# A hybrid of eight residual layers: the third normalization merged into linear attention, and the rings of PSUM tiles changed in two kinds of feed-forward

## Chip, cores, metric

The kernel runs on one core of one Trainium2 chip. The metric is the device time of one execution in microseconds (us), lower is better; a time given for the kernel is the median of several runs.

## The reference, cut to what matters

The input x has 8 sequences of 512 tokens with 128 channels. Eight residual layers follow, each on a layer normalization of x. The change touches the second, third, fourth, sixth and eighth:

```python
x = x + L0_attn_a(layernorm(x))          # state space scan
x = x + L0_ffn(layernorm(x))             # quantized feed-forward
x = x + L0_attn_b(layernorm(x))          # linear attention
x = x + L0_ffn(layernorm(x))
x = x + L1_attn_a(layernorm(x))          # forgetting attention
x = x + L1_ffn(layernorm(x))             # einsum with sign(weight)
x = x + L1_attn_b(layernorm(x))          # rotary attention
x = x + L1_ffn(layernorm(x))

# L0_ffn: every product of fp4_linear quantizes its input in blocks of 16
scale = max(abs(xb)) / 6; q = grid[searchsorted(mid, abs(xb / scale))] * sign * scale
h = silu(fp4_linear(x, w_gate)) * fp4_linear(x, w_up); y = fp4_linear(h, w_down)   # 128 -> 352 -> 128
# L0_attn_b: no softmax
att = (0.1 * x @ Wq) @ (0.1 * x @ Wk).T; att = att * causal - (1 - causal)
att = att / (sum(att) + 1e-5); y = att @ (x @ Wv) @ Wo + bo
```

## The kernel before

x lives in SBUF for the whole kernel as X, channels on the 128 partitions, [batch, token] along them. The program is a row of stages, one after the other. Each `Stage` opens its own SBUF and PSUM tiles and semaphores, and ends with clearing the semaphores and a barrier of all engines; inside it each engine runs its instructions in the order in which the code writes them, and waits on semaphores alone. No planner and no pool decides anything. All data here are 32-bit floats; such a matmul shows as two records on PE (TensorE). PSUM has eight banks of 512 floats a partition, and each stage divides them by hand.

`layernorm_stage`: `center(n)` is a matmul with I - 1/128 for batch n into a ring of six banks, `keep(n)` copies it to XN on VectorE (DVE), ScalarE (ACT) squares it; `variance(k)` brings four batches' means into one bank, 32 rows each; ScalarE's `root(k)` and VectorE's three-step `refine(k)` make `fine`, 1/sqrt; `widen(k)` spreads it to all channels with four matmuls of 32 rows, and VectorE's `scale(n)` multiplies XN by it.

`linear_attention_stage`: for each of the 8 batches PE computes `tokens_up`, `values`, four blocks of `scores`, `outputs` and `turn` (a transpose). ScalarE copies from PSUM, GpSimd (POOL) puts -1 where a token must not look, VectorE divides by the row sum and adds the residual. PE's order interleaves batch i's outputs with batch i+1's scores.

`ffn0_stages` works on tokens on the partitions. Its front normalizes and quantizes X: a pair of batches is 1024 floats a partition, so two banks. Three such places make the ring `cps`, two more banks are `qps`. `center(g)` is called for g = 0 to 3 (the statistics: `moments` on ScalarE, `block_maxima` on VectorE) and a second time for g = 4 to 7, since three places can't hold four pairs until their scales are known. Then each pair goes through `code_scaled`, `sizes` (ScalarE), `code_total`, `minus_code`, GpSimd's product (line 1018), `back` (transposes on PE) and `out` into XQ. The last call waits for a place:

```python
for g in range(BATCHES + RING):
    center(g)
center(BATCHES + RING)
back(0)
back(1)
```

The main loop then runs over 16 pairs of 128-token tiles: `gates`, `ups_of` on PE, `product`, `maxima`, `scales`, `scaled`, `total` on VectorE, sizes on ScalarE, two pairs of products on GpSimd (lines 1023, 1026), `turn` and `down` on PE, and a `residual` on VectorE in every other pair from the sixth on. gates, ups and transposes take the ring's PSUM again.

`norm_ffn1_stage` never stores the normalized x: `center(n)` into one of two banks, a square on ScalarE, `variance`, `root`, `refine`; meanwhile `signed(n)`, a matmul with the centered sign matrix `mix`, into the same two banks, `keep(n)` on ScalarE copies it, `widen(k)` spreads four batches' 1/sqrt over four banks, VectorE's `scale(n)` multiplies and GpSimd adds to X. In the last stage SP (the DMA queue) sends X out by twos.

## Time and profile before

| | us |
|---|---|
| median of 3 runs (2116.9 to 2118.9) | 2117.75 |
| the profiled execution's own time | 2115.72 |
| its span in the trace | 2113.9 |
| first quantized feed-forward, from its first matmul to the next stage's first | 381.1 to 509.4 |
| third normalization | 509.4 to 529.5 |
| linear attention | 529.5 to 594.3 |
| second quantized feed-forward | 594.3 to 721.1 |
| sign-mixed stages | 1708.7 to 1738.4 and 2082.6 to the end |

Times in the trace are us from the span's start. A stage starts where the one before has ended on all engines, so what a stage saves the kernel saves, and waits inside one stage do not reach into another.

### The profile page before, as it was taken

What the parts mean: (1) busy time and instruction counts of PE and PEld (TensorE: products, weight loads), DVE (VectorE), ACT (ScalarE), POOL (GpSimd) and SP (SyncE); (2) the same over time, 40 slices, a digit from 0 to 9 for tenths busy, and PEclk for the clock granted to TensorE, in tenths of its full rate; (3) what the DMA queues carried; (4) which work ended last, traced back from release to release, by engine and by line L of the source; (5) the groups of instructions that cost most, each with busy time, mean ns of one, the idle gap of its engine ahead of it and who ended that gap; (6) DMA issues with size and microseconds to landing.
All of it is one profiled execution on the core that took longest, in us unless ns stands there. A gap on an engine that the chain in (4) does not pass through costs nothing. (4 is left out here: it accounts for less than half of the span.)

```text
span 2113.9 us, 36196 instructions
## 1 busy us (share of the span) xinstructions
PE 1808.2 (86%) x11955; PEld 870.2 (41%) x11955; DVE 1683.8 (80%) x2282; ACT 1404.3 (66%) x2314; POOL 1042.6 (49%) x1138
## 2 busy tenths in 40 slices
PE   4558887687978769999999999999999867789996
PEld 2213332543764314555555555555554423222222
DVE  5979997796369669888888888888887637798884
ACT  2547775575357547777777777777776534789994
POOL 0067775174217435776666666776666521431112
PEclk9869999798999879999999999999999979999999
DMA  3000000000000021111121111112121100422211
GB/s 98 0 15 0 0 0 0 1 1 1 2 1 1 0 74 49 59 60 61 54 63 64 60 54 61 64 60 61 53 63 63 37 16 25 96 83 52 61 46 40
DMA packets 71437, 84.54 MB, mean 40 GB/s; under 512 B 20544, under 2 KB 44032, under 8 KB 71168
## 3 DMA queue, kind: packets, MB, share of 16 engines
q1 hardware_dynamic: 69536, 81.69, 12.8%
q8 instruction: 94, 1.54, 0.3%
q10 hardware_dynamic: 1728, 0.67, 0.1%
q14 instruction: 79, 0.65, 0.1%
HBM read 71.95 MB, written 9.57 MB: 39 GB/s over the span
## 5 line engine op out<-in xcount | busy, mean ns | idle before, releaser
L1806 DVE SCALAR_TENSOR_TENSOR fu_kv<-fu_ps_kv,fa_vec,fu_kv 128x511 f32<-128x511 f32 (+2 forms) x384 | 285.8, 746 | 55.7 <-ACT fu_kv L1678 50.7
L1889 POOL TENSOR_TENSOR fu_ds<-fu_p 128x768 f32<-128x768 f32 x64 | 115.8, 1809 | 191.6 <-PE fu_ps_ss L1577 191.4
L2244 ACT ACTIVATE rt_p<-rt_ps_s 128x1024 f32<-128x1024 f32 x192 | 185.6, 1029 | 25.1 <-PE rt_ps_s L2175 25.1
L1537 PE MATMUL fu_ps_s<-fu_qn,fu_kn 64*128 64x512 f32 (+3 forms) x1024 | 190.0, 468 | 2.2 <-DVE fu_sg L1767 1.4
L625 POOL TENSOR_TENSOR scan_hC<-scan_h,scan_c 128x1024 f32<-128x1024 f32 x64 | 150.9, 2358 | 71.7 <-DVE scan_h L601 71.7
L1678 ACT ACTIVATE fu_kv<-fu_ps_kv,fa_vec 128x512 f32<-128x512 f32 x128 | 88.3, 690 | 110.9 <-PE fu_ps_kv L1586 67.0
L1567 PE MATMUL fu_ps_n<-fu_p,fu_vt 128*64 128x512 f32 (+3 forms) x1024 | 151.9, 439 | 0.0
L524 PE MATMUL scan_ps_y<-scan_hC,w_ident 128*128 128x512 f32 x256 | 125.8, 614 | 26.3 <-POOL scan_hC L625 14.8
L601 DVE TENSOR_TENSOR_SCAN scan_h<-scan_dA,scan_ps_b 128x1024 f32<-128x1024 f32 x64 | 146.4, 2287 | 2.2
L2140 POOL TENSOR_SCALAR rt_d<-rt_d 128x1024 f32<-128x1024 f32 x32 | 35.0, 1094 | 184.0 <-DVE rt_d L2265 178.3
L1905 POOL TENSOR_TENSOR fu_kn<-fu_ks,fu_rb 128x512 f32<-128x512 f32 x64 | 81.6, 1275 | 71.0 <-DMA fu_rb<-rms_rows 70.7
L1682 ACT ACTIVATE fu_ps_kv<-fu_kv 128x512 f32<-128x512 f32 x128 | 77.0, 602 | 55.8 <-DVE fu_kv L1806 55.6
L1537 PEld LDWEIGHTS fu_ps_s<-fu_qn,fu_kn 64*128 64x128 f32 x1024 | 82.9, 185 | 74.6 <-issue 55.7
L571 ACT ACTIVATE scan_c<-scan_ps_c 128x1024 f32<-128x1024 f32 x64 | 65.6, 1024 | 67.4 <-PE scan_ps_c L545 49.1
L2189 PE MATMUL rt_ps_o<-rt_p,rt_va 128*32 128x512 f32 x768 | 103.3, 610 | 7.0 <-ACT rt_p L2244 5.6
L567 ACT ACTIVATE scan_dA<-ssm_delta,w_decay 128x511 f32 (+1 forms) x128 | 85.1, 716 | 13.2 <-DVE scan_dA L587 13.0
L2175 PE MATMUL rt_ps_s<-ra_stackq,ra_stackk 48*128 48x512 bf16 x512 | 84.5, 391 | 6.3 <-PEq L75 5.7
L1567 PEld LDWEIGHTS fu_ps_n<-fu_p,fu_vt 128*64 128x64 f32 x1024 | 63.4, 136 | 63.4 <-issue 60.2
L1909 POOL TENSOR_TENSOR fu_num<-fu_num,fu_sg 128x512 f32<-128x512 f32 x64 | 82.6, 1291 | 9.9 <-DVE fu_sg L1767 9.8
L1893 POOL TENSOR_TENSOR fu_ds<-fu_ds,fu_p 128x512 f32<-128x512 f32 x64 | 82.3, 1285 | 5.0
L1586 PE MATMUL fu_ps_kv<-w_XN,fa_wp 128*128 128x512 f32 x128 | 74.4, 664 | 11.7 <-PEq L75 8.7
L1023 POOL TENSOR_TENSOR ff_q<-ff_tot,ff_mag 128x352 f32<-128x352 f32 x64 | 59.8, 935 | 47.5 <-DVE ff_tot L990 47.5
(387 smaller groups left out, 5277.7 us busy)
## 6 DMA issues: line engine op xcount, KB each, us to landing
fu_rb<-rms_rows SPq DMA_DIRECT2D x256, 128.0 KB, 2.9
fu_ro<-rms_rows SPq DMA_DIRECT2D x128, 128.0 KB, 3.0
ra_stackq<-rope_parts SPq DMA_DIRECT2D x168, 32.0 KB
ra_stackk<-rope_parts SPq DMA_DIRECT2D x168, 32.0 KB
w_X<-in_xT SPq DMA_DIRECT2D x4, 512.0 KB, 6.9
fa_wp<-in_wp SPq DMA_DIRECT2D x8, 256.0 KB
fa_cr<-ncum_rows SPq DMA_DIRECT2D x128, 3.0 KB
rope_parts<-ra_hi SPq DMA_DIRECT2D x16, 128.0 KB, 2.7
```

The costliest lines, as they stand in the source:

```text
L524: i = pe.matmul(yps[:, :], w.ident[:, :], hC[p % (BEHIND + 2)][:, j, :], start=(p == 0 and j == 0), stop=False)
L567: m = act.activation(dA[p % 2][:, j, 1:T], DL[:, n, 1:T], ACT.Exp, scale=w.decay[:, k:k + 1])
L601: dve.tensor_tensor_scan(flat[0], flat[1], flat[2], 0.0, ALU.mult, ALU.add).then_inc(s.scan, 1)
L625: pool.tensor_tensor(hC[p % (BEHIND + 2)][:, :, :], hst[p % 2][:, :, :], csb[p % 2][:, :, :], ALU.mult).then_inc(s.hC, 1)
L1537: pe.matmul(sps[:, h, at:at + T - t * P], k[head(h), t * P:(t + 1) * P], q[head(h), t * P:T], start=(at == 0), stop=False)
L1567: m = pe.matmul(nps[head(h), t * P:T], VT[p % VR][:, t, head(h)], e[:, h, :], start=(t == 0), stop=(t == 2))
L1678: act.activation(KV[:, at, :], kvps[:, at, :], ACT.Copy, scale=vec[:, a % GA, last:last + 1]).then_inc(done, 1)
L1806: dve.scalar_tensor_tensor(acc, kvps[:, at, 0:T - j], vec[:, a % GA, w:w + 1], acc, ALU.mult, ALU.add).then_inc(done, 1)
L1889: pool.tensor_tensor(DS[:, :, :], P0[p % 2][:, :, P:T], P13[:, :, 0:3 * P], ALU.add).then_inc(s.d1, 1)
L2175: m = pe.matmul(sps[u % RING][:, e, :], stack[1][rows, pair, t * P:(t + 1) * P], stack[0][rows, pair, :], start=True, stop=True)
L2189: m = pe.matmul(ops[32 * j:32 * j + 32, :], va[n % 2][:, t, 4 * q4 + j, :], p[j // 2][:, j % 2, :], start=(t == 1), stop=(t == 0))
L2244: act.activation(p[:, :, :], sps[unit(g, t, i) % RING][:, :, :], ACT.Exp, scale=DH_B ** -0.5).then_inc(s.exp, 1)
```

## The change

Four edits.

In `ffn0_stages` the ring `cps` has four places, all eight banks, so each pair is centered once and stays. `qps` has no banks of its own any more: it is the two halves of the place that is free first. The pairs are coded in the order 3, 2, 0, 1 (`ORDER`), which lets gates, ups and transposes keep places 2, 0 and 1; `PLACES` gives the batch at each position in XQ and X.

In the same stage `scaled` and `total` read their factor 1.0 from a column of constants in SBUF, `w.one`, where it was an immediate.

`linear_attention_stage` does the third normalization itself: the `ln3` stage is gone from the list, with its barrier. The first four batches are scaled before `tokens_up(0)`, the others after (`widen(4)` behind the first scores, `widen(5)` to `widen(7)` within the first batch's outputs).

In `norm_ffn1_stage` the ring for `center` and `signed` has four banks instead of two, the widened rows two instead of four; `widen` goes by pairs, each square has its own tile.

The quantized feed-forward:
```diff
-            RING = 3
-            cps = [st.ps(f"c{k}", [P, NB, FQ]) for k in range(RING)]
-            qps = [st.ps(f"q{k}", [P, T]) for k in range(2)]
+            ORDER = (3, 2, 0, 1)
+            PLACES = [2 * k + j for k in ORDER for j in range(2)]
+            cps = [st.ps(f"c{k}", [P, NB, FQ]) for k in range(BATCHES)]
+            qps = [cps[ORDER[0]][:, j * NB // 2:(j + 1) * NB // 2, :].rearrange("p a q -> p (a q)") for j in range(2)]
...
-                    def center(g):
-                        k, before = g % BATCHES, g - RING
-                        if before >= BATCHES:
-                            pe.wait_ge(c.q, before - BATCHES + 1)
-                        elif before >= 0:
-                            pe.wait_ge(c.sq, TOK * (before + 1))
-                            pe.wait_ge(c.amax, before + 1)
+                    def center(k):
                         for t in range(TOK):
                             n, at = 2 * k + t // NT, t % NT * P
-                            m = pe.matmul(cps[g % RING][:, t * XB:(t + 1) * XB, :].rearrange("p a q -> p (a q)"), X[:, n, at:at + P], w.center[:, :], start=True, stop=True)
+                            m = pe.matmul(cps[k][:, t * XB:(t + 1) * XB, :].rearrange("p a q -> p (a q)"), X[:, n, at:at + P], w.center[:, :], start=True, stop=True)
                         m.then_inc(c.cent, 1)
...
-                    for g in range(BATCHES + RING):
-                        center(g)
-                    center(BATCHES + RING)
+                    for k in range(BATCHES):
+                        center(k)
                     back(0)
                     back(1)
...
-                        xn = cps[(BATCHES + k) % RING][:, :, :]
+                        xn = cps[ORDER[k]][:, :, :]
                         dve.wait_ge(c.both, 2 * k // BATCHES + 1)
-                        dve.wait_ge(c.cent, BATCHES + k + 1)
-                        dve.tensor_tensor(xn, xn, widen(both[:, k, :], FQ), ALU.mult).then_inc(c.xn, 1)
+                        dve.wait_ge(c.cent, BATCHES)
+                        dve.tensor_tensor(xn, xn, widen(both[:, ORDER[k], :], FQ), ALU.mult).then_inc(c.xn, 1)
...
-                        dve.scalar_tensor_tensor(hk, hk, 1.0, widen(inv[k % 4][:, :, :].rearrange("p e a -> p (e a)"), FQ), ALU.mult, ALU.mult).then_inc(s.xn, 1)
+                        dve.scalar_tensor_tensor(hk, hk, w.one[:, 0:1], widen(inv[k % 4][:, :, :].rearrange("p e a -> p (e a)"), FQ), ALU.mult, ALU.mult).then_inc(s.xn, 1)
...
-                        dve.scalar_tensor_tensor(tot[k % 2][:, :, :, :], mag[k % 2][:, :, :, :], 1.0, h[k % 3][:, :, :, :], ALU.mult, ALU.add).then_inc(s.tot, 1)
+                        dve.scalar_tensor_tensor(tot[k % 2][:, :, :, :], mag[k % 2][:, :, :, :], w.one[:, 0:1], h[k % 3][:, :, :, :], ALU.mult, ALU.add).then_inc(s.tot, 1)
```

The linear attention (`variance`, `square`, `root`, `keep` and `refine` are as in `layernorm_stage`, with a tile of its own for each square):
```diff
+        ups, vps, more = st.ps("u", [P, T]), st.ps("v", [P, T]), st.ps("n", [P, T])
         aps = [st.ps(f"a{k}", [P, T]) for k in range(2)]
-        yps = [st.ps(f"y{k}", [P, P + 1]) for k in range(2)]
+        yps = [st.ps(f"y{k}", [P, T]) for k in range(2)]
         tps = st.ps("t", [P, T])
-        s = st.sems("ones u v uc vc a ac mask two three y rs ri yt t x")
+        ring = [ups, aps[0], aps[1], tps, yps[0], yps[1]]
+        spread = [vps, more]
+        wide = [yps[0], yps[1], tps, aps[1]] + [more] * HALF
+        s = st.sems("cent kept sq var lnv rstd vr vrr fine wide norm ones u v uc vc a ac mask two three y rs ri yt t x")
...
+                def center(n):
+                    pe.wait_ge(s.kept, max(n - HALF - 1, 0))
+                    pe.matmul(ring[n % (HALF + 2)][:, :], w.center[:, :], X[:, n, :], start=True, stop=True).then_inc(s.cent, 1)
+
...
+                def widen(n):
+                    pe.wait_ge(s.fine, n // HALF + 1)
+                    pe.wait_ge(s.kept, B)
+                    if n > HALF:
+                        pe.wait_ge(s.norm, n)
+                    row = 32 * (n % HALF)
+                    rows = slice(row, row + 32)
+                    pe.matmul(wide[n][:, :], w.rowsel[rows, :], fine[n // HALF][rows, :], start=True, stop=True).then_inc(s.wide, 1)
...
                     pe.wait_ge(s.uc, i)
+                    pe.wait_ge(s.norm, i + 1)
...
+                for n in range(HALF + 2):
+                    center(n)
+                variance(0)
+                for n in range(HALF + 2, B):
+                    center(n)
+                variance(1)
+                for n in range(HALF):
+                    widen(n)
                 tokens_up(0)
                 values(0)
                 for k in range(NT):
                     scores(0, k)
+                widen(HALF)
...
                         if ahead:
                             scores(i + 1, t - 1)
+                        if i == 0:
+                            widen(HALF + t)
                         turn(i, t - 1)
...
+                def scale(n):
+                    dve.wait_ge(s.wide, n + 1)
+                    dve.wait_ge(s.sq, n + 1)
+                    dve.tensor_tensor(XN[:, n, :], XN[:, n, :], wide[n][:, :], ALU.mult).then_inc(s.norm, 1)
+
+                for n in range(B):
+                    keep(n)
+                refine(0)
+                for n in range(HALF):
+                    scale(n)
+                refine(1)
+                scale(HALF)
...
+                        if i == 0 and t:
+                            scale(HALF + t)
...
-            lambda: layernorm_stage(nc, "ln3", w, X, XN), lambda: linear_attention_stage(nc, w, X, XN),
+            lambda: linear_attention_stage(nc, w, X, XN),
```

The sign-mixed stage:
```diff
-        cps = [st.ps(f"c{k}", [P, T]) for k in range(2)]
-        rps = [st.ps(f"r{k}", [P, T]) for k in range(HALF)]
+        cps = [st.ps(f"c{k}", [P, T]) for k in range(HALF)]
+        rps = [st.ps(f"r{k}", [P, T]) for k in range(2)]
         mix = st.sb("mix", [P, P])
...
-                    pe.wait_ge(s.sq, max(n - 1, 0))
-                    pe.matmul(cps[n % 2][:, :], w.center[:, :], X[:, n, :], start=True, stop=True).then_inc(s.cent, 1)
+                    pe.wait_ge(s.sq, max(n - HALF + 1, 0))
+                    pe.matmul(cps[n % HALF][:, :], w.center[:, :], X[:, n, :], start=True, stop=True).then_inc(s.cent, 1)
...
-                def widen(k):
-                    pe.wait_ge(s.fine, k + 1)
-                    pe.wait_ge(s.scaled, HALF * k)
-                    for j in range(HALF):
-                        rows = slice(32 * j, 32 * j + 32)
-                        m = pe.matmul(rps[j][:, :], w.rowsel[rows, :], fine[k][rows, :], start=True, stop=True)
+                def widen(pair):
+                    pe.wait_ge(s.fine, pair // 2 + 1)
+                    pe.wait_ge(s.scaled, 2 * pair)
+                    for j in range(2):
+                        row = 32 * (2 * (pair % 2) + j)
+                        rows = slice(row, row + 32)
+                        m = pe.matmul(rps[j][:, :], w.rowsel[rows, :], fine[pair // 2][rows, :], start=True, stop=True)
                     m.then_inc(s.wide, 1)
 
                 def signed(n):
-                    pe.wait_ge(s.sq, B)
-                    pe.wait_ge(s.kept, max(n - 1, 0))
-                    pe.matmul(cps[n % 2][:, :], mix[:, :], X[:, n, :], start=True, stop=True).then_inc(s.y, 1)
+                    pe.wait_ge(s.sq, min(HALF + n + 1, B))
+                    pe.wait_ge(s.kept, max(n - HALF + 1, 0))
+                    pe.matmul(cps[n % HALF][:, :], mix[:, :], X[:, n, :], start=True, stop=True).then_inc(s.y, 1)
 
                 pe.matmul(vps[0][:, 0:P], w.center[:, :], w.signT[:, :], start=True, stop=True).then_inc(s.mixp, 1)
-                for n in range(HALF):
+                for n in range(HALF + 2):
                     center(n)
-                center(HALF)
                 variance(0)
-                for n in range(HALF + 1, B):
+                for n in range(HALF + 2, B):
                     center(n)
+                signed(0)
+                signed(1)
                 variance(1)
-                for n in range(B):
-                    signed(n)
-                    if n == 1 or n == HALF + 1:
-                        widen(n // HALF)
+                signed(2)
+                widen(0)
+                signed(3)
+                widen(1)
+                signed(4)
+                signed(5)
+                widen(2)
+                signed(6)
+                signed(7)
+                widen(3)
 
...
-                    act.activation(sq[n % HALF][:, :], cps[n % 2][:, :], ACT.Square).then_inc(s.sq, 1)
+                    act.activation(sq[n][:, :], cps[n % HALF][:, :], ACT.Square).then_inc(s.sq, 1)
...
-                    dve.wait_ge(s.wide, n // HALF + 1)
-                    dve.tensor_tensor(ys[:, n, :], ys[:, n, :], rps[n % HALF][:, :], ALU.mult).then_inc(s.scaled, 1)
+                    dve.wait_ge(s.wide, n // 2 + 1)
+                    dve.tensor_tensor(ys[:, n, :], ys[:, n, :], rps[n % 2][:, :], ALU.mult).then_inc(s.scaled, 1)
...
-                for n in range(HALF):
-                    scale(n)
-                    if n == 1:
-                        refine(1)
-                for n in range(HALF, B):
+                scale(0)
+                scale(1)
+                refine(1)
+                for n in range(2, B):
                     scale(n)
```

How the instructions stand on the engines. First PE in the front of the first quantized feed-forward, before (`w_center` is the centering matrix, L758 is `back`, L768 `gates`, L774 `ups_of`):
```order
L749 MATMUL ff_ps_c<-w_center,w_X 128x128 x64
L758 MATMUL ff_ps_q<-w_ident,ff_cxq 128x128 x16
L768 MATMUL ff_ps_c<-w_gate,ffn_xq 128x352 x2
L774 MATMUL ff_ps_c<-w_up,ffn_xq 128x352 x2
L758 MATMUL ff_ps_q<-w_ident,ff_cxq 128x128 x8
L768 MATMUL ff_ps_c<-w_gate,ffn_xq 128x352 x2
L758 MATMUL ff_ps_q<-w_ident,ff_cxq 128x128 x8
```
and of the change:
```order
L744 MATMUL ff_ps_c<-w_center,w_X 128x128 x32
L753 MATMUL ff_ps_c<-w_ident,ff_cxq 128x128 x16
L763 MATMUL ff_ps_c<-w_gate,ffn_xq 128x352 x2
L769 MATMUL ff_ps_c<-w_up,ffn_xq 128x352 x2
L753 MATMUL ff_ps_c<-w_ident,ff_cxq 128x128 x8
L763 MATMUL ff_ps_c<-w_gate,ffn_xq 128x352 x2
L753 MATMUL ff_ps_c<-w_ident,ff_cxq 128x128 x8
```
32 centering matmuls less, and no other instruction of PE moved; lines 753, 763 and 769 are the same three functions.

Next PE in the linear attention, around the first `outputs`, before (L1068 `scores`, L1057 `tokens_up`, L1076 and L1080 `outputs`, L1062 `values`, L1086 `turn`):
```order
L1068 MATMUL la_ps_a<-w_XN,la_uT 128x384
L1068 MATMUL la_ps_a<-w_XN,la_uT 128x256
L1068 MATMUL la_ps_a<-w_XN,la_uT 128x128
L1057 MATMUL la_ps_u<-w_XN,w_u 128x512
L1076 MATMUL la_ps_y<-la_v,la_at 128x129
L1080 MATMUL la_ps_y<-la_later,w_neg 128x129
L1062 MATMUL la_ps_v<-w_vo,w_XN 128x128 x4
L1076 MATMUL la_ps_y<-la_v,la_at 128x129 x2
L1080 MATMUL la_ps_y<-la_later,w_neg 128x129
L1068 MATMUL la_ps_a<-w_XN,la_uT 128x512
L1086 MATMUL la_ps_t<-w_ident,la_y 128x128
```
and of the change (L1074 is `widen`, into `la_ps_n`):
```order
L1091 MATMUL la_ps_a<-w_XN,la_uT 128x128
L1074 MATMUL la_ps_n<-la_fine,w_rowsel 128x512
L1079 MATMUL la_ps_u<-w_XN,w_u 128x512
L1099 MATMUL la_ps_y<-la_v,la_at 128x129
L1103 MATMUL la_ps_y<-la_later,w_neg 128x129
L1084 MATMUL la_ps_v<-w_vo,w_XN 128x128 x4
L1099 MATMUL la_ps_y<-la_v,la_at 128x129 x2
L1103 MATMUL la_ps_y<-la_later,w_neg 128x129
L1091 MATMUL la_ps_a<-w_XN,la_uT 128x512
L1074 MATMUL la_ps_n<-la_fine,w_rowsel 128x512
L1109 MATMUL la_ps_t<-w_ident,la_y 128x128
L1099 MATMUL la_ps_y<-la_v,la_at 128x129 x3
```
A widening stands ahead of the second `tokens_up`, and one between `scores` and `turn`; two more follow in the same way behind these rows.

Last PE in the sign-mixed stage, before (L1175 `center`, L1181 `variance`, L1195 `signed`, L1189 `widen`):
```order
L1175 MATMUL sf_ps_c<-w_X,w_center 128x512 x5
L1181 MATMUL sf_ps_v<-sf_sq,w_ones_mean 32x512 x4
L1175 MATMUL sf_ps_c<-w_X,w_center 128x512 x3
L1181 MATMUL sf_ps_v<-sf_sq,w_ones_mean 32x512 x4
L1195 MATMUL sf_ps_c<-w_X,sf_mix 128x512 x2
L1189 MATMUL sf_ps_r<-sf_fine,w_rowsel 128x512 x4
L1195 MATMUL sf_ps_c<-w_X,sf_mix 128x512 x4
L1189 MATMUL sf_ps_r<-sf_fine,w_rowsel 128x512 x4
L1195 MATMUL sf_ps_c<-w_X,sf_mix 128x512 x2
```
and of the change (L1253 `center`, L1259 `variance`, L1274 `signed`, L1268 `widen`):
```order
L1253 MATMUL sf_ps_c<-w_X,w_center 128x512 x6
L1259 MATMUL sf_ps_v<-sf_sq,w_ones_mean 32x512 x4
L1253 MATMUL sf_ps_c<-w_X,w_center 128x512 x2
L1274 MATMUL sf_ps_c<-w_X,sf_mix 128x512 x2
L1259 MATMUL sf_ps_v<-sf_sq,w_ones_mean 32x512 x4
L1274 MATMUL sf_ps_c<-w_X,sf_mix 128x512
L1268 MATMUL sf_ps_r<-sf_fine,w_rowsel 128x512 x2
L1274 MATMUL sf_ps_c<-w_X,sf_mix 128x512
L1268 MATMUL sf_ps_r<-sf_fine,w_rowsel 128x512 x2
L1274 MATMUL sf_ps_c<-w_X,sf_mix 128x512 x2
L1268 MATMUL sf_ps_r<-sf_fine,w_rowsel 128x512 x2
L1274 MATMUL sf_ps_c<-w_X,sf_mix 128x512 x2
```
Six centers come ahead of the first variance, two `signed` ahead of the second, and the widenings stand in four pairs.

## Rows read from the trace of the kernel before

**Rows 1.** The page, part 1: busy time, share of the span and instructions of each engine.
```profile
PE 1808.2 (86%) x11955; PEld 870.2 (41%) x11955; DVE 1683.8 (80%) x2282; ACT 1404.3 (66%) x2314; POOL 1042.6 (49%) x1138
```

**Rows 2.** Stretches: length; busy time (instructions) of PE, PEld, DVE, ACT, POOL; granted clock.
```profile
381.10:417.20 36.10, 24.99 (x155) 22.49 (x156) 22.97 (x29) 23.00 (x81) 7.67 (x8) 0.81 0.00 1
...
529.50:594.20 64.70, 61.85 (x384) 48.04 (x384) 26.79 (x104) 23.15 (x48) 16.18 (x50) 0.96 0.00 1
2082.60:2113.90 31.30, 19.88 (x66) 6.29 (x66) 10.56 (x15) 13.04 (x21) 10.45 (x8) 0.91 0.17 67
```

**Rows 3.** Timeline, first quantized feed-forward: start, length, engine, operation, [idle before <- releaser].
```profile
404.67 3.77 PE L749 MATMUL ff_ps_c<-w_center,w_X 128*128 128x128 f32 x16 [8.11 <-DVE ff_cq L949]
...
408.54 1.23 DVE L939 TENSOR_TENSOR ff_ps_c<-ff_ps_c,ff_both 128x1024 f32<-128x1024 f32 x1 [2.79 <-PE ff_ps_c L749]
...
412.09 2.13 PE L758 MATMUL ff_ps_q<-w_ident,ff_cxq 128*128 128x128 f32 x8 [2.78 <-POOL ff_cxq L1018]
...
417.19 0.89 DVE L968 TENSOR_TENSOR ff_h<-ff_gt,ff_ps_c 128x704 f32<-128x704 f32 x1 [1.50 <-PE ff_ps_c L774]
```

**Rows 4.** Stretches, columns as in rows 2; the granted clock is the third last.
```profile
404.70:408.20 3.50, 3.50 (x16) 3.50 (x17) 1.05 (x1) 1.15 (x1) 2.07 (x2) 0.50 0.00 0
412.10:415.10 3.00, 3.00 (x10) 2.28 (x11) 2.97 (x3) 1.52 (x3) 2.69 (x3) 0.50 0.00 0
...
529.50:534.50 5.00, 4.98 (x12) 3.21 (x13) 0.00 (x0) 1.20 (x2) 0.56 (x4) 0.50 0.00 2
```

**Rows 5.** Timeline of the first feed-forward's main loop.
```profile
437.84 1.06 DVE L985 SCALAR_TENSOR_TENSOR ff_h<-ff_h,ff_inv 128x704 f32<-128x704 f32 x1
...
438.23 1.31 POOL L1026 TENSOR_TENSOR ff_hq<-ff_q,ff_above 128x352 f32<-128x352 f32 x1
...
438.82 1.47 DVE L990 SCALAR_TENSOR_TENSOR ff_tot<-ff_mag,ff_h 128x704 f32<-128x704 f32 x1
...
444.60 0.88 DVE L990 SCALAR_TENSOR_TENSOR ff_tot<-ff_mag,ff_h 128x704 f32<-128x704 f32 x1
```

**Rows 6.** Groups by shape on DVE: busy us, mean ns | idle before.
```profile
L1849 DVE SCALAR_TENSOR_TENSOR fu_qn<-fu_qs,fu_qw,fu_rb 128x512 f32<-128x512 f32 x64 | 48.7, 761 | 0.0
...
L216 DVE SCALAR_TENSOR_TENSOR ln_v<-ln_v,ln_rstd 128x512 f32<-128x512 f32 x8 | 5.5, 692 | 0.3
```

**Rows 7.** Timeline, forgetting attention, DVE and POOL.
```profile
1690.67 1.27 POOL L1909 TENSOR_TENSOR fu_num<-fu_num,fu_sg 128x512 f32<-128x512 f32 x1 [1.49 <-DVE fu_sg L1767]
...
1691.11 1.38 DVE L1774 SCALAR_TENSOR_TENSOR fu_og<-fu_num,fu_ow,fu_ro 128x512 f32<-128x512 f32 x1
```

**Rows 8.** Timeline, third normalization and linear attention.
```profile
520.63 1.85 PE L173 MATMUL ln_ps_b<-ln_fine,w_rowsel 32*128 32x512 f32 x8 [0.39 <-DVE ln_fine L218]
...
523.81 3.67 DVE L222 TENSOR_TENSOR w_XN<-w_XN,ln_ps_b 128x512 f32<-128x512 f32 x6
...
529.52 2.05 PE L1057 MATMUL la_ps_u<-w_XN,w_u 128*128 128x512 f32 x2 [3.48 <-PEq L75]
...
537.32 0.39 PE L1076 MATMUL la_ps_y<-la_v,la_at 128*128 128x129 f32 x2
...
543.61 1.02 PE L1057 MATMUL la_ps_u<-w_XN,w_u 128*128 128x512 f32 x2
...
544.47 0.27 PE L1086 MATMUL la_ps_t<-w_ident,la_y 128*128 128x128 f32 x1
```

**Rows 9.** Timeline, last sign-mixed stage.
```profile
2082.94 4.65 PE L1175 MATMUL sf_ps_c<-w_X,w_center 128*128 128x512 f32 x10
...
2092.91 1.06 PE L1181 MATMUL sf_ps_v<-sf_sq,w_ones_mean 128*32 128x512 f32 x8 [0.69 <-ACT sf_sq L1218]
...
2095.82 1.14 PE L1189 MATMUL sf_ps_r<-sf_fine,w_rowsel 32*128 32x512 f32 x8
...
2097.10 1.29 DVE L1255 TENSOR_TENSOR sf_ys<-sf_ys,sf_ps_r 128x512 f32<-128x512 f32 x2 [4.31 <-PE sf_ps_r L1189]
...
2104.83 4.94 POOL L1272 TENSOR_TENSOR w_X<-w_X,sf_ys 128x512 f32<-128x512 f32 x4 [0.21 <-DVE sf_ys L1255]
```

86 lines of the change are left out of this document (59 added, 27 removed).

## The prediction, as made before the result was known

> **What bounds the kernel now.** I read the page's totals first. TensorE is busy 86% of the span and VectorE 80% [rows 1], which says no more than that no one engine bounds all of it: the program is a row of stages with a barrier between each two, and a stage is as long as the last wait in it. So I read next the table of stretches [rows 2] for the stages that the edit touches. In the front part of the quantized feed-forward, PE is busy 25.0 of 36.1 us, VectorE and ScalarE 23 each: nobody is full, so waits set its length. In the linear attention PE is busy 61.9 of 64.7 us: it is bound by TensorE. In the last sign-mixed stage PE is busy 19.9 of 31.3 us, the others less: waits again. Then I read each of these places instruction by instruction.
>
> Front of the feed-forward [rows 3]: PE sits idle 8.11 us until VectorE's `minus_code(0)` lets go of a ring place, then computes the last centered pair a second time (16 records, 3.77 us), and VectorE sits idle 2.79 us for it before `code_scaled(3)`. It is a ring of three places for four pairs that makes this wait.
>
> Seam into the linear attention [rows 8]: `widen` starts at 520.63, VectorE scales from 523.81 to the stage's end, PE starts `tokens_up(0)` at 529.52 and `outputs(0, 0)` at 537.32; from there it hardly stops.
>
> Sign-mixed stage [rows 9]: the first scale waits for the first widened rows (2097.10), these for `widen(0)` at 2095.82, which stands on PE behind two rounds through two PSUM tiles; GpSimd adds the residual as scaled pieces come, the last four from 2104.83 in 4.94 us.
>
> **The change part by part.**
>
> *Four pairs in PSUM, both feed-forward stages.* 32 of 64 centering matmuls go. Those that were recomputed early ran under other work and bring nothing; the last group's 2.79 us idle does count [rows 3]. With it gone `code_scaled(3)` follows `code_total(1)` at once, and `minus_code` 1 to 3, GpSimd's products behind them, `back(1)`, `gates(0)`, `ups_of(0)` and the first product of the main loop (417.19) all hang on it. ScalarE is then late next: its `sizes(3)` stands behind `out(0)`, which waits for GpSimd; that takes some 0.6 us of the gain from `minus_code(3)`, but the first product waits for PE, not for that. I take 2.8 us a stage. What could eat it is PE's clock. In the stretch of recomputation it was granted 0.50, the 1.2 GHz level, and again from 412.10, after a pause, for 3 us of full work [rows 4]. `back(1)`, with which PE's unbroken work starts, begins in that same state now and then, so the same pattern moves forward as a whole; if PE needs longer, the first gates and ups run at half speed and up to 1.7 us of each 2.8 is lost. Bounds: 1.1 and 2.8 a stage; I take 2.8, since the slow stretch is in the trace of before already. Two stages: -5.6.
>
> *Normalization merged.* All is as before until `widen(0)` at 520.63. Before, both `refine` steps came ahead of all scales, then a barrier. Now `scale(0)` follows the four widened pieces (1.85 us, to 522.5) and ends 0.7 later; `tokens_up(0)` starts at 523.2 instead of 529.52. From its start to `outputs(0, 0)` took 7.80 us [rows 8], 5 of them at 0.50 clock [rows 4]; I keep that, since PE comes out of the same slow stretch. Into this goes `widen(4)`, 0.86 us (the step from one such matmul pair to the next instruction, 543.61 to 544.47, [rows 8]). So `outputs(0, 0)` comes at 531.9, 5.4 earlier. But three more widenings now stand between PE's instructions in the first batch, where PE is full: 3 x 0.86 = 2.6 us back, since alone they don't share the array as four in a row do (1.14 us for four, [rows 9]). The three scales on VectorE are covered: it is busy 26.8 of 64.7 us [rows 2]. Net -2.8. Bounds: if PE is at full clock from the start, the 7.8 shrinks to some 5.3 (5 us at half speed are 2.5 at full), net -5.3; if each switch between whole-array and 32-row matmuls costs the 0.28 by which four (1.14) exceed one (0.86), twice for each of four, +2.2, net -0.6.
>
> The Trainium skill has a rule on that (TensorEngine Tiling (Array Packing), Key Properties): changing the tiling mode drains TensorE. It gives no price; by it the split widenings, here and in the sign-mixed stage, cost more than their own length, and the lower bound just worked out would be the one to take, a time some 2 us above mine; its chance is in rival 1.
>
> *Four-place ring in the sign-mixed stage, twice.* Center matmuls no longer wait for squares two behind. Counting PE's queue in the last stage from 2082.94 with 0.86 a matmul and 1.0 for a `variance` (1.06 with its tail, [rows 9]): eight centers, two `variance`, three `signed` give 2082.94 + 11 x 0.86 + 2.0 = 2094.4 for `widen(0)`, against 2095.82. The first variance comes 0.6 later (six centers ahead of it, not five), which costs nothing: `fine(0)` is ready before `widen(0)`'s turn. A pair of widenings is shorter than four by some 0.1, so VectorE's first scale comes 1.5 to 1.6 earlier. `refine(1)`, with GpSimd's adds in its way as before, moves along. The widening in pairs lets scales 4 and 5 come 1.8 earlier, and 6 and 7 0.7 to 1.0 earlier, but GpSimd is behind by then: its adds run without pause from 2104.83, and that start moves by 1.6. The output's DMAs hang on these adds. -1.6 a stage, -3.2 for two; bounds 0.6 (if the last widening sets the end) and 1.9.
>
> *1.0 read from a column instead of an immediate*, in `scaled` and `total` (lines 985 and 990), 64 instructions in all. The trace has no such form of the same shape; the nearest rows: with a per-partition scalar a 512-wide instruction takes 761 ns, with a constant 692 [rows 6]: 0.07 more. But most of these 64 are held up by GpSimd anyway: `scaled` 1.06 instead of 0.88, GpSimd's product behind it 1.31 instead of 0.79, `total` 1.47 [rows 5]. A held instruction of the scalar-column form [rows 7] starts at 1691.11, GpSimd's product ends at 1691.94, and it ends at 1692.49: 0.55 us later, and 512 elements alone take 0.53. So its extra hides in the wait. Uncovered are about ten a stage (the first pairs, and `total` behind a residual, 0.88 at 444.60 [rows 5]): 20 x 0.07 = +1.3. Bounds: 0, and all 64, +4.5.
>
> By the Trainium skill (SBUF — State Buffer, SBUF: two separate sides) a VectorE instruction with two SBUF inputs and a GpSimd one take a shared pair of ports as an exclusive lock; [rows 5] and [rows 7] agree, and so the form of the scalar would change nothing of the loop's 0.75 us of waiting a pair.
>
> *Renamed places* (`PLACES`, `ORDER`) only permute; nothing to cost. The memory roles of gates, ups and transposes are the same PSUM pairs.
>
> **Sum:** -5.6 - 2.8 - 3.2 + 1.3 = -10.3 us. The profiled execution took 2115.72 us around its 2113.9 us span, 2.0 below the median of the runs shown (2117.75); the sum against it gives 2105.4, and beside the median 2107.4. The latter is what I predict. A measurement of this kernel can tell 0.2%, 4.2 us, from no change.
>
> **Rivals.**
>
> 1. *The clock keeps the merge and the fronts from paying* (0.16). PE starts the merged attention and the first gates at 1.2 GHz for longer, since the matmuls that kept it busy are gone. For it: 0.50 granted in each of those stretches [rows 4]. Against it: they were slow before the change too. Fronts -1.1 each, merge -0.6: -2.2 - 0.6 - 3.2 + 1.3 = -4.7, 2113.
>
> 2. *The scalar column spoils the loop's rhythm* (0.07; the other side). `scaled` slips in between two GpSimd products today; if its later request for the ports lets GpSimd's second product go first and `total` then meets the third, a pair costs another 0.58 us (`total`'s 1.47 against 0.88, [rows 5]). 32 pairs: up to +18.6, with the rest -11.6: 2124.8. From 0.36 us a pair on the gain is gone. Against it: by [rows 7] the form queues like the other.
>
> 3. *The scalar column frees the ports* (0.04): the 0.75 us a pair of held time ((1.06 - 0.88) + (1.47 - 0.88) = 0.77, [rows 5]) would go, -24: about 2082. Against it: [rows 7].
>
> 4. *The change does not do what it says* (0.05): the first product of the loop or GpSimd's adds wait for something that does not move, only the merge pays: -2.8 + 1.3, 2116.
>
> The forecast itself has 0.68: from 2102 (full clock in the merge, -5.3, and 1.9 twice in the mixed stage, no cost of the column, some luck) to 2110.
>
> **How the numbers follow.** 2107.4 is the likeliest. The range takes in rival 1 nearly whole: 2102 to 2113. Faster by over 0.2% (below 2113.5): 0.68 + 0.16 + 0.04, less the rim of rival 1, plus the mild half of rival 2: 0.89. Within 0.2%: 0.07 (rival 4 and what rival 2 leaves). Slower: 0.04.
>
> **What the changed kernel's profile would show.** VectorE's idle time before the fourth code scaling gone, and the loop's first product some 36.1 - 2.8 us after the stage's first matmul. `outputs(0, 0)` 22.5 us after the merged stage's first matmul, not 27.9; the first batch on PE 9.8 us long, not 7.3. GpSimd's last four adds 20.6 us after the last stage's start, not 22.2. `scaled` and `total` at 1.06 and 1.47 in the even pairs still. I am wrong if the loop's pairs change length, if a single widening costs clearly over 0.86, or if PE's granted clock falls where it now stands at full.

## The result, and the profile after

The changed kernel took 2107.01 us (median of 7 runs, 2102.2 to 2111.8), the kernel before 2117.75: a ratio of 0.9945, interval 0.9934 to 0.9957. A second series of the same two gave 0.9950 (0.9936 to 0.9963). The forecast was 2107.4, in a range of 2102 to 2113, and faster by 10.3 us. The total is right. Its terms are not: in the profiles the stages that the change touches are 2.8 us shorter, not 10.3.

The profiled execution took 2110.68 us around a span of 2108.7 (before 2115.72 and 2113.9), so the two profiles differ by 5.2 us and not by 10.7: the one of the kernel before is 2.0 under its median, this one 3.7 over its own. The second profile of the changed kernel, an execution of 2107.76 us, is at its median. Busy time of the whole page:
```profile
PE 1797.7 (85%) x11827; PEld 859.5 (41%) x11827; DVE 1685.7 (80%) x2282; ACT 1403.4 (67%) x2314; POOL 1041.1 (49%) x1138
```
PE lost 128 records (two a matmul) and 10.5 us of work against [rows 1], the others hardly anything. The length of each stage is read from the timeline of PE, from the stage's first matmul to the next stage's first:

| us | before | after | after, second profile |
|---|---|---|---|
| first quantized feed-forward | 128.3 | 127.5 | 127.2 |
| third normalization and linear attention | 84.9 | 83.2 | 83.2 |
| second quantized feed-forward | 126.8 | 127.5 | 127.4 |
| forgetting attention (not edited) | 955.2 | 952.1 | 949.8 |
| first, second sign-mixed stage | 29.6, 31.3 | 29.3, 30.6 | 29.1, 30.6 |
| all others (not edited) | 757.8 | 758.5 | 758.0 |

The front of the first feed-forward in the timeline, to lay beside [rows 3]:
```profile
406.44 1.22 DVE L934 TENSOR_TENSOR ff_ps_c<-ff_ps_c,ff_both 128x1024 f32<-128x1024 f32 x1
...
406.58 2.13 PE L753 MATMUL ff_ps_c<-w_ident,ff_cxq 128*128 128x128 f32 x8 [15.43 <-POOL ff_cxq L1013]
...
409.97 2.13 PE L753 MATMUL ff_ps_c<-w_ident,ff_cxq 128*128 128x128 f32 x8 [1.26 <-POOL ff_cxq L1013]
...
411.90 2.50 PE L763 MATMUL ff_ps_c<-w_gate,ffn_xq 128*128 128x352 f32 x4
...
414.24 1.35 PE L769 MATMUL ff_ps_c<-w_up,ffn_xq 128*128 128x352 f32 x4
...
415.68 0.89 DVE L963 TENSOR_TENSOR ff_h<-ff_gt,ff_ps_c 128x704 f32<-128x704 f32 x1 [1.71 <-PE ff_ps_c L769]
```
VectorE's 2.79 us wait before the fourth code scaling is gone, as forecast: from the first code scaling to `back(1)` it now takes 12.1 us (397.87 to 409.97), before 15.0 (397.09 to 412.09). But the first product comes 34.76 us after the stage's first matmul, not 33.3. Stretches of the changed kernel with the granted clock third from last, beside [rows 4]: the stage's start, the transposes and gates, the merged attention's start, and the start of the second feed-forward.
```profile
381.00:386.00 5.00, 5.00 (x24) 5.00 (x25) 0.00 (x0) 2.45 (x12) 0.00 (x0) 0.50 0.01 3
406.60:413.50 6.90, 5.64 (x19) 4.05 (x20) 6.53 (x6) 4.38 (x7) 5.09 (x5) 0.50 0.00 1
520.20:526.00 5.80, 5.58 (x19) 3.01 (x13) 4.52 (x7) 1.08 (x3) 0.00 (x0) 0.50 0.01 3
591.90:594.90 3.00, 3.00 (x16) 3.00 (x16) 0.00 (x0) 0.97 (x1) 0.00 (x0) 0.50 0.01 3
```
All four run at the 1.2 GHz level, 0.50. Before, PE had been recomputing ahead of its transposes; now it has sat idle for 15.43 us, and the gates take 2.50 us instead of 1.90. In the kernel before:
```profile
414.02 1.90 PE L768 MATMUL ff_ps_c<-w_gate,ffn_xq 128*128 128x352 f32 x4
...
415.75 1.35 PE L774 MATMUL ff_ps_c<-w_up,ffn_xq 128*128 128x352 f32 x4
```
The stage's start is slower too. The same stretch in the changed kernel and in the kernel before:
```profile
384.50:386.80 2.30, 2.30 (x12) 2.30 (x12) 0.00 (x0) 2.09 (x16) 0.00 (x0) 0.50 0.03 7
```
```profile
384.50:386.80 2.30, 2.30 (x23) 2.30 (x23) 0.00 (x0) 2.05 (x17) 0.00 (x0) 1.00 0.03 7
```
The first code scaling comes 16.95 us after the first matmul instead of 15.95. So of the 2.9 us of wait 1.0 goes at the start and 0.6 behind `back(1)`. In the second feed-forward the start is at 0.50, where the kernel before had 1.00: ScalarE's first square comes 3.69 us after the first matmul, before 2.06, and the first product at 34.73, before 34.52. There the start takes 1.6 us and the stretch behind `back(1)` 1.5, and nothing is left.

The main loop, to lay beside [rows 5]:
```profile
436.44 1.06 DVE L980 SCALAR_TENSOR_TENSOR ff_h<-ff_h,w_consts,ff_inv 128x704 f32<-128x704 f32 x1
...
436.82 1.31 POOL L1021 TENSOR_TENSOR ff_hq<-ff_q,ff_above 128x352 f32<-128x352 f32 x1
...
437.42 1.47 DVE L985 SCALAR_TENSOR_TENSOR ff_tot<-ff_mag,w_consts,ff_h 128x704 f32<-128x704 f32 x1
...
443.19 0.94 DVE L985 SCALAR_TENSOR_TENSOR ff_tot<-ff_mag,w_consts,ff_h 128x704 f32<-128x704 f32 x1
```
The held instructions are as before, 1.06 and 1.47 (1.31 on GpSimd between them); the uncovered `total` behind a residual takes 0.94, not 0.88. From first to last product the loop takes 73.9 us, before 73.5, in each of the two stages.

The merged attention, beside [rows 8] (the stage's first matmul is at 508.42):
```profile
522.17 2.05 PE L1079 MATMUL la_ps_u<-w_XN,w_u 128*128 128x512 f32 x2 [0.22 <-DVE w_XN L1209]
...
530.98 0.39 PE L1099 MATMUL la_ps_y<-la_v,la_at 128*128 128x129 f32 x2
...
532.99 1.02 PE L1091 MATMUL la_ps_a<-w_XN,la_uT 128*128 128x512 f32 x2
...
533.94 1.12 PE L1074 MATMUL la_ps_n<-la_fine,w_rowsel 32*128 32x512 f32 x2
...
535.00 0.33 PE L1109 MATMUL la_ps_t<-w_ident,la_y 128*128 128x128 f32 x1
...
541.84 0.39 PE L1099 MATMUL la_ps_y<-la_v,la_at 128*128 128x129 f32 x2
```
`outputs(0, 0)` comes 22.56 us after the first matmul; forecast 22.5. The first batch takes 10.86 us, to 541.84, before 7.26. A widening set between other matmuls takes 1.06 us to the next instruction, and the `scores` ahead of it 0.95 where it took 0.86 before, the `turn` behind it 0.16 instead of 0.11: 1.20 in all, three times, which is the 3.6 us.

The last sign-mixed stage, beside [rows 9] (first matmul at 2078.10):
```profile
2090.32 1.13 PE L1268 MATMUL sf_ps_r<-sf_fine,w_rowsel 32*128 32x512 f32 x4
...
2091.57 1.28 DVE L1338 TENSOR_TENSOR sf_ys<-sf_ys,sf_ps_r 128x512 f32<-128x512 f32 x2 [3.21 <-PE sf_ps_r L1268]
...
2099.26 2.49 POOL L1354 TENSOR_TENSOR w_X<-w_X,sf_ys 128x512 f32<-128x512 f32 x2 [0.18 <-DVE sf_ys L1338]
...
2100.23 1.13 PE L1268 MATMUL sf_ps_r<-sf_fine,w_rowsel 32*128 32x512 f32 x4
...
2102.24 2.48 POOL L1354 TENSOR_TENSOR w_X<-w_X,sf_ys 128x512 f32<-128x512 f32 x2 [0.49 <-DVE sf_ys L1338]
```
`widen(0)` comes at 12.22 us, before 13.18; forecast 11.76. The eleven whole-array matmuls ahead of it take 9.9 us, not 11 x 0.86 = 9.5; the `signed` alone between `variance` and the widening takes 1.06. GpSimd's adds now go by twos, and it idles 0.49 before the last two, whose scales wait for the fourth widening at 2100.23. The last four start 1.0 us earlier after the stage's first matmul (21.16 against 22.19; forecast 20.6), and the stage ends 0.7 earlier.

### The profile page after: what moved, and what is told of

The parts are those of the page before. It is cut to its first block and busy times, and to the rows that moved or that the text cites. A ratio compares the mean times of both kernels' runs of the same rounds, so it can differ in the third digit from the quotient of the medians.

```text
span 2108.7 us, 35923 instructions
## 1 busy us (share of the span) xinstructions
PE 1797.7 (85%) x11827; PEld 859.5 (41%) x11827; DVE 1685.7 (80%) x2282; ACT 1403.4 (67%) x2314; POOL 1041.1 (49%) x1138
## 5 line engine op out<-in xcount | busy, mean ns | idle before, releaser
L524 PE MATMUL scan_ps_y<-scan_hC,w_ident 128*128 128x512 f32 x256 | 125.7, 614 | 26.4 <-POOL scan_hC L625 14.9
L1668 PE MATMUL fu_ps_kv<-w_XN,fa_wp 128*128 128x512 f32 x128 | 73.5, 656 | 12.4 <-PEq L75 9.1
```

The lines of the kernel that those rows point to most:

```text
L524: i = pe.matmul(yps[:, :], w.ident[:, :], hC[p % (BEHIND + 2)][:, j, :], start=(p == 0 and j == 0), stop=False)
```

## The experiments

All ratios are against the kernel before, run on the same chip. The kernels a to d make one part of the change each. Lengths of stages and times of first products are from the one profiled execution of each kernel, the medians from all its runs.

**a: the ring alone.**
```diff
-            RING = 3
+            ORDER = (3, 2, 0, 1)
...
+                    for k in range(BATCHES):
+                        center(k)
```


> Only the four-place ring of the quantized feed-forward, with the factor 1.0 left an immediate. By the prediction's sum both stages lose 2.8 us: VectorE's idle time before the fourth code scaling goes and the first product of the main loop comes 33.3 us after the first stage's first matmul, 31.7 after the second's; ratio 0.9974. The rival, from the trace of the changed kernel: the granted clock takes back what the wait gave. PE now pauses some 15 us before the first transposes and runs them and the first gates at 0.50, and where a stage also starts at 0.50 the first centered pair comes 1.6 us later; then the first product comes at 34.7 in each stage, -1.3 in the first and nothing in the second, ratio 0.9994.

Measured: 2111.2 us, 0.9975 (0.9966 to 0.9984). The first product comes 33.70 and 33.10 us after the stage's first matmul, before 36.05 and 34.52. Its second feed-forward started at full clock, and its timeline shows what the prediction lost:
```profile
616.06 2.13 PE L753 MATMUL ff_ps_c<-w_ident,ff_cxq 128*128 128x128 f32 x8 [15.73 <-POOL ff_cxq L1013]
...
619.45 2.13 PE L753 MATMUL ff_ps_c<-w_ident,ff_cxq 128*128 128x128 f32 x8 [1.26 <-POOL ff_cxq L1013]
...
621.38 2.55 PE L763 MATMUL ff_ps_c<-w_gate,ffn_xq 128*128 128x352 f32 x4
...
623.72 2.24 PE L769 MATMUL ff_ps_c<-w_up,ffn_xq 128*128 128x352 f32 x4
...
626.05 0.89 DVE L963 TENSOR_TENSOR ff_h<-ff_gt,ff_ps_c 128x704 f32<-128x704 f32 x1 [2.61 <-PE ff_ps_c L769]
```
```profile
621.40:625.40 4.00, 4.00 (x8) 2.33 (x8) 2.01 (x2) 1.36 (x3) 3.29 (x4) 0.50 0.00 0
```
The second `back` comes 12.1 us after the first code scaling here too, so the wait gives 2.9. But the gates and the ups take 2.55 and 2.24 us, nearly all of it at the lower level (the ups above, at full clock, 1.35); from `back(1)` to the product it takes 6.60 us, before 5.1. Of the 2.9 us 1.4 are left.

**b: the merge alone.**
```diff
-            lambda: layernorm_stage(nc, "ln3", w, X, XN), lambda: linear_attention_stage(nc, w, X, XN),
+            lambda: linear_attention_stage(nc, w, X, XN),
```


> Only the third normalization merged into linear attention. By the prediction's sum -2.8 us, 0.9987: first outputs 22.5 us after the merged stage's first matmul, then a first batch of 9.8. The changed kernel's trace had 22.6 and 9.9, but the stage as a whole was only 1.7 us shorter than the two before; by that 0.9992, and the first matmul of the second feed-forward 83.2 us behind the merged stage's. The rival: the second feed-forward starts at another granted clock because the merge moved it; then its first product comes at 36.1 and not 34.5 us after the stage's first matmul, and the merge brings nothing, 1.0000.

Measured: 2113.9 us, 0.9977 (0.9968 to 0.9986). Stretches of its trace, the merged stage's start and the second feed-forward's:
```profile
520.00:529.00 9.00, 7.40 (x35) 3.69 (x36) 6.53 (x10) 4.70 (x9) 1.93 (x4) 1.00 0.00 0
591.30:595.00 3.70, 3.69 (x19) 3.70 (x20) 0.00 (x0) 1.36 (x2) 0.00 (x0) 0.57 0.01 2
```
Here the merged stage runs at 1.00 and takes 80.5 us, `outputs(0, 0)` at 19.83: 4.4 us gained. The second feed-forward begins at 0.50, and takes 128.3 instead of 126.8. So the same code is worth 4.4 or 1.7 us, by the clock, and 1.5 go back in the next stage. Forgetting attention is 4.2 us shorter (951.0); by what is shown under k and l.

**c: the sign-mixed ring alone.**
```diff
-        cps = [st.ps(f"c{k}", [P, T]) for k in range(2)]
+        cps = [st.ps(f"c{k}", [P, T]) for k in range(HALF)]
```


> Only the four-bank ring in the two sign-mixed stages. By the prediction's sum -1.6 us a stage, 0.9985. The rival, from the changed kernel's trace: the last widening has taken over as the last wait, GpSimd idles before its last two adds, and a stage gives 0.4 to 0.7 us: 0.9995, last stage 30.6 us from its first matmul to the end.

Measured: 2118.9 us, 1.0005 (0.9996 to 1.0014). The last stage takes 30.6 us, the first 27.6. The first stage's early stretch, here and in the changed kernel:
```profile
1710.70:1713.70 3.00, 3.00 (x9) 1.56 (x10) 0.29 (x1) 2.39 (x3) 0.00 (x0) 1.00 0.01 3
```
```profile
1704.50:1707.00 2.50, 2.50 (x5) 0.95 (x4) 0.00 (x1) 1.05 (x2) 0.00 (x0) 0.50 0.01 3
```
It is 1.7 us shorter where it starts at 1.00 (27.6) than with the same code at 0.50 (29.3). The 2.7 us that both stages give in this profile don't show in the median, and forgetting attention is 1.8 us longer (957.0).

**d: the column alone.**
```diff
-dve.scalar_tensor_tensor(hk, hk, 1.0, ...
+dve.scalar_tensor_tensor(hk, hk, w.one[:, 0:1], ...
```


> Only the factor 1.0 read from a column of constants in the feed-forward's scaled and total. By the prediction +1.3 us in all; from the changed kernel's trace, where the loop from its first to its last product is 73.9 us and not 73.5, +0.8: ratio 1.0004 to 1.0006. The rival, which would explain a gain of the whole change larger than the touched stages show: the form of the scalar changes something outside these stages and the kernel is faster by itself, 0.997 or less.

Measured: 2123.4 us, 1.0029 (1.0017 to 1.0040). Loops of 73.9 us, stages of 129.6 and 128.2 (before 128.3, 126.8): 2.6 us of the 5.5. Only 0.8 of them are in the loops. In the first stage 0.8 come before the first product (36.82 for 36.05), where no edited instruction has run; with the same front b, c, i, k and l have 36.5 to 37.6. In the second 1.0 comes behind the last product: PE's next-to-last `down` starts under a lower clock that lasts longer, and takes 5.49 us where it took 4.34.
```profile
711.80:717.20 5.40, 5.40 (x7) 2.19 (x8) 1.40 (x1) 0.66 (x1) 5.20 (x6) 0.50 0.00 0
```
Another 2.4 stand in forgetting attention (957.6 for 955.2).

**The changed kernel again, and with the immediate.** The second kernel undoes d's edit in the changed kernel.

> The changed kernel once more, unaltered, to see how far one program's untouched stages differ from execution to execution. If the length of forgetting attention (955.2, 952.2, 952.6, 951.0, 957.0, 957.6 us in six traces, though no edit touches it) is chance, this profile can show anything from 951 to 958 and the ratio stays 0.9945 within 0.001. If it belongs to the program, it shows 952.2 again.

> The changed kernel with the factor 1.0 as an immediate again in the feed-forward. If the column costs only what the loop shows (73.9 instead of 73.5 us from first to last product, and about 0.1 at the loop's end), this is 1.0 us faster than the changed kernel, 0.9940. If the column costs what its own run showed (0.9 to 1.3 us in each of these stages, 1.0029 for the whole), it is 3 to 6 us faster, 0.992. By the prediction 1.3.

Measured: 2107.8 us, 0.9950 (0.9936 to 0.9963), and 2106.4 us, 0.9948 (0.9934 to 0.9961). Forgetting attention: 949.8 and 949.7. The loops are 73.5 us with the immediate, so the column costs 0.8 us in two stages; the medians, with intervals of 0.13% (2.8 us) either way, can neither show that nor rule out 3 us. The other 1.8 us of d's two stages are not the column's: they stand where no edited instruction has run, and in a `down` at the lower clock.

**i: a delay alone.**
```diff
+                    for k in range(2):
+                        dve.scalar_tensor_tensor(pad[k][:, :], XQ[:, k, :], 1.0, XQ[:, k + 2, :], ALU.mult, ALU.add)
```


> The kernel before, with two instructions of 512 elements added on VectorE at the end of each quantized feed-forward, whose results nobody reads: 1.4 us longer stages, as the column alone made them 1.3 longer, but with nothing of the column. If the column's 1.0029 is its stages' 2.7 us and a shift of all that follows, this gives the same: 1.0025 to 1.003. If it is the stages' time alone, 1.0013, and the rest of the column's cost lies in its own form.

Measured: 2123.5 us, 1.0028 (1.0018 to 1.0039). The same ratio as d, but not in the same places: forgetting attention is 955.1 as before. Each delay costs its own 1.4 to 1.7 us, and 1.7 more in the normalization behind it (21.8 us for 20.1). PE sits idle 2.96 us at the barrier, not 1.76, and its next matmuls run at the lower level:
```profile
511.75 6.66 PE L159 MATMUL ln_ps_b<-w_X,w_center 128*128 128x512 f32 x11 [2.96 <-PEq L75]
```
```profile
511.80:514.00 2.20, 2.20 (x3) 0.89 (x4) 0.50 (x1) 1.19 (x1) 0.00 (x0) 0.57 0.00 0
```
The kernel before, in the same place:
```profile
509.40:512.40 3.00, 2.97 (x7) 1.44 (x8) 1.50 (x3) 2.15 (x3) 0.00 (x0) 1.00 0.00 0
```
So the equal ratio doesn't bear out that a shift explains d.

**g and h: PE kept busy in the front.** Both start from the kernel with the immediate and repeat the centering of place 1 (six times, eight times); h also has six small matmuls around the last `turn` of the linear attention, whose results nobody reads, and `signed(6)` and `signed(7)` ahead of `widen(2)`.
```diff
+                    for k in range(WARM):
+                        center(1)
                     back(0)
```


> The same as the kernel with the immediate, and PE repeats the centering of place 1 six times into the same place between the statistics and the first transposes (96 matmuls, some 14 us of PE's 15.4 us pause), with the fourth code scaling waiting for them. If the granted clock is what took back part of the ring's gain, the first transposes and gates run at 1.00, the first product comes 31 us after the stage's first matmul where the stage starts at full clock and 32.5 where not, and a stage is 1.5 to 2.4 us shorter: 0.9922 with the immediate's 0.9940. If the pause isn't what lowers the clock, or the wait for the ready products is what sets the first product, nothing changes; if the repeats collide with the others' reads, it is slower.

Measured: 2107.9 us, 0.9949 (0.9935 to 0.9963). First products at 33.51 and 34.75, as with the immediate alone (33.41, 34.71). The repeats ended early, and after a pause of 4.4 us the transposes ran at 0.50:
```profile
401.00:405.00 4.00, 0.00 (x0) 0.00 (x0) 4.00 (x4) 2.94 (x4) 0.77 (x1) 1.00 0.00 0
405.40:411.90 6.50, 5.24 (x19) 3.74 (x20) 6.13 (x6) 4.34 (x6) 4.86 (x5) 0.50 0.00 1
```


> The kernel with six repeats again, but with eight, since six ended 4.4 us before the first transposes and the clock had fallen back to 0.50 by then; besides, six matmuls of 128 columns on PE around the last turn of the linear attention (results not read), and in the sign-mixed stage both last signed products ahead of the third widening. If the granted clock is what holds the fronts: transposes, gates and ups of the first feed-forward run at 1.00 and its first product comes 31 us after the stage's first matmul instead of 33.5; the second feed-forward starts at 1.00, squares 2.1 us after its first matmul instead of 3.7, and its first product at 31 instead of 34.7; whole 2100 to 2102, 0.992. If something else holds the first product, 33.4 and 34.7 stay and the ratio is 0.9948. The sign-mixed stages give 0.4 us each in either case.

Measured: 2106.5 us, 0.9951 (0.9937 to 0.9965). The rows are the repeats, `back(0)`, `back(1)` with the gates, and the second feed-forward's start:
```profile
391.00:405.60 14.60, 14.50 (x128) 14.37 (x128) 12.59 (x20) 10.11 (x31) 0.22 (x1) 1.00 0.01 1
406.50:408.50 2.00, 1.31 (x8) 0.83 (x8) 2.00 (x2) 0.94 (x3) 0.96 (x1) 1.00 0.00 0
409.90:415.00 5.10, 5.10 (x14) 3.55 (x15) 3.55 (x3) 2.79 (x4) 4.46 (x5) 0.50 0.00 0
589.60:592.60 3.00, 2.99 (x27) 3.00 (x28) 0.00 (x0) 2.18 (x9) 0.00 (x0) 1.00 0.03 8
```
Now `back(0)` runs at 1.00, but PE then waits for GpSimd's product, and the clock has fallen when `back(1)` starts at 409.89: the first product comes at 34.69. In the second feed-forward, which starts at 1.00, it comes at 32.30 and the stage takes 124.6 us, 2.7 less than with the immediate alone. The other order was a miss: 31.7 us for the last stage, 30.6 without it; that the third widening now stands behind two more signed products is the likely reason, not tested alone.

**n: only the small matmuls at the attention's end.**
```diff
+                pe.wait_ge(s.uc, B)
+                for k in range(2):
+                    pe.matmul(ups[:, 0:P], w.u0[:, :], XN[:, 0, 0:P], start=True, stop=True)
                 turn(B - 1, NT - 1)
+                for k in range(4):
+                    pe.matmul(ups[:, 0:P], w.u0[:, :], XN[:, 0, 0:P], start=True, stop=True)
```


> The changed kernel with the immediate, and only the six matmuls of 128 columns around the last turn of the linear attention (results not read) added. In the kernel with eight repeats they went with a second feed-forward that started at 1.00: squares 2.06 us after its first matmul instead of 3.69. If they are what keeps the clock, the same here, the second feed-forward's first product at 33.1 instead of 34.7 and the stage 125.5 instead of 127.3 us; whole about 1.7 us below the immediate's 2106.4, 0.994. If it was the repeats in the first feed-forward that moved the clock's steps, 3.69 and 34.7 stay.

Measured: 2106.0 us, 0.9942 (0.9930 to 0.9954). The second feed-forward's start, and the last stage's:
```profile
588.50:591.50 3.00, 2.98 (x27) 3.00 (x27) 0.00 (x0) 2.18 (x8) 0.00 (x0) 1.00 0.03 8
2071.00:2075.00 4.00, 3.11 (x7) 1.55 (x8) 0.29 (x1) 1.88 (x2) 0.00 (x0) 0.74 0.00 0
```
The second feed-forward starts at 1.00, its first product comes at 32.02 and it takes 124.2 us, 3.0 less than with the immediate alone. The linear attention is at full clock too (80.6 for 83.2), though the edit stands at its end, so the clock's steps had moved for another reason as well. That is 5.6 us gained, and the total is the same: forgetting attention took 953.0 (949.7 with the immediate alone), the first feed-forward 126.8 (125.7), and both sign-mixed stages, unchanged code, ran longer at the lower level near their start and took 30.6 and 32.3 (29.3 and 30.6), as they did in g (30.5 and 32.3).

**k and l: an empty stage ahead.** One put ahead of the merged attention (on b), one ahead of the third normalization (on the kernel before).
```diff
+            lambda: empty_stage(nc, w, X), lambda: linear_attention_stage(nc, w, X, XN),
```


> The merge alone, with an empty stage (one wait, its clearing of semaphores and its barrier) put in front of the linear attention, where the third normalization's end stood. Five traces with the merge show forgetting attention at 949.7 to 952.2 us, five without it at 952.6 to 957.6, though no edit touches it. If the number of instructions ahead of it (a stage's end less) makes that difference, it goes back to about 955 here and the ratio to 0.9995; if the merge acts otherwise, or the difference is chance, it stays near 951 and the ratio is the merge's 0.9977 plus the 2 to 3 us of the empty stage, 0.9988.

> The kernel before with the same empty stage in front of the third normalization. If forgetting attention's length depends on where its instructions lie in the stream, it moves away from 955.2 here by a few us either way; if not, it is 955 and the kernel is slower by the empty stage's 2 to 3 us alone, 1.0012.

Measured: k 2116.8 us, 0.9999 (0.9990 to 1.0008), forgetting attention 955.4; l 2120.8 us, 1.0016 (1.0006 to 1.0025), forgetting attention 956.1. By the medians the empty stage costs 0.0022 on b and 0.0016 on the kernel before, and the difference, 1.3 us, is within the intervals; b's profiled execution was also the fastest of its 11. The medians settle nothing. The traces do, when forgetting attention is compared record by record. Here is one place of it in the kernel before, in b and in k:
```profile
1015.31 1.27 POOL L1893 TENSOR_TENSOR fu_ds<-fu_ds,fu_p 128x512 f32<-128x512 f32 x1
1015.46 1.16 DVE L1792 TENSOR_SCALAR fu_root<-fu_var 96x64 int32<-96x64 int32 x1 [0.65 <-DMA fu_var<-fu_ms]
```
```profile
1013.11 0.19 DVE L1875 TENSOR_SCALAR fu_root<-fu_var 96x64 int32<-96x64 int32 x1 [0.30 <-DMA fu_var<-fu_ms]
...
1013.31 1.27 POOL L1976 TENSOR_TENSOR fu_ds<-fu_ds,fu_p 128x512 f32<-128x512 f32 x1
```
```profile
1017.19 1.27 POOL L1987 TENSOR_TENSOR fu_ds<-fu_ds,fu_p 128x512 f32<-128x512 f32 x1
...
1017.33 1.18 DVE L1886 TENSOR_SCALAR fu_root<-fu_var 96x64 int32<-96x64 int32 x1 [0.64 <-DMA fu_var<-fu_ms]
```
In b VectorE's small instruction starts 0.20 us before GpSimd's product and takes 0.19 us. Where its data land 0.35 us later it starts behind that product and lasts until the product is over, 1.16 us, and PE's next matmuls come 1.6 us later. Such steps, of about 1.6 us and each with a `fu_root` that runs into a GpSimd product, stand at fixed places in the stage (numbers are PE's records in it, 7808 in all):

| profiles | steps near record | 500th to 7300th record, us |
|---|---|---|
| before, a, c, d, i | 2006, 4446, 6642 | 778.8 to 779.7 |
| k | 2006, 4446, 6642 | 779.3 |
| b, e | none | 775.0 |
| changed kernel (twice), g, h, n | 3959 | 776.2 to 777.5 |
| l | 786, 4934, 5422 | 779.0 |

The empty stage puts k's steps back where the kernel before has them, and moves all three of them in l. So they hang on what stands ahead in the program, and not on the number of stages alone, since e and the changed kernel differ only in the form of a scalar. Why the data land later at these places is open.

The second feed-forward starts at 0.50 in k and in l too, and takes 128.8 and 128.5 us; l has no merge:
```profile
597.30:600.50 3.20, 3.20 (x17) 3.20 (x16) 0.00 (x0) 1.24 (x8) 0.00 (x0) 0.50 0.00 0
```

## Why the prediction was right, and where it was not

**Four pairs in PSUM, -5.6.** The wait was right (2.9 us instead of 2.8 a stage). The step that failed is "I take 2.8, since the slow stretch is in the trace of before already". The slow stretch did not move forward as a whole: without the recomputation PE is idle for 15 us, and is at 0.50 through the gates and in the second stage through the ups, which makes the way from `back(1)` to the product 0.2 and 1.5 us longer in a, 0.6 and 1.5 in the full change. By the products of kernel a the term is -2.3 and -1.4, together -3.7. The first is taken from single profiles that scatter: without the ring seven traces have that product at 36.05 to 37.6 us (mean 36.7), with it and without repeats five have it at 33.4 to 34.8 (mean 34.2), so -2.5 is the better value. In the full change the product moves by -1.3 and +0.2 against the kernel before, since there the stages' starts are slower by 1.0 and 1.6 us as well, which the prediction did not price; against b, whose second feed-forward starts at the same low level (product at 35.98), the second is -1.3. This is rival 1's mechanism, near its size (-1.1) in the second stage. That the pause alone decides it is not shown: with PE at work up to `back(0)` (h) the second stage's product comes at 32.30, and without that work, from the same full-clock start, at 32.02 (n) or 33.10 (a). When the clock comes back behind the pause differed from trace to trace.

**Merged normalization, -2.8.** The start was right to 0.1 us (22.56 for 22.5). The term mis-sized is 0.86 for a single widening: it took 1.20. In the full change the stage gives -1.7, between the bound with the dearer switch (-0.6) and the value taken. The case of the bound with full clock (-5.3) was seen as well, in b, h and n: -4.2 to -4.4. By the Trainium skill (TensorEngine Tiling (Array Packing), Key Properties) changing the tiling mode drains TensorE; the 0.34 us beyond 0.86 agree with it. What was not seen at all is the stage behind: in each of the five traces with the merge and without the small matmuls or the empty stage the second feed-forward starts at 0.50, in the kernel before, a, c, d and i at 1.00. That is +1.5. The merge is not the only thing that does it, since l starts at 0.50 without it; and in h and n, with PE busy until 1.0 us before the stage, it starts at 1.00. What decides the level there is open.

**Sign-mixed ring, -3.2.** The sum took the start of GpSimd's last four adds as what sets the end. It is the last widening, the case of the bound 0.6: -0.4 and -0.7 measured, and -2.1 in c's first stage, where 1.7 are the clock's. The start too moved by 1.0 and not by 1.6, since PE's queue of eleven matmuls was priced 0.5 us too short.

**Column, +1.3.** Right by mechanism and nearly by size: held instructions unchanged, uncovered ones 0.06 to 0.07 us dearer, +0.8 in the two loops. (20 x 0.07 is 1.4; the sum has 1.3.) Rivals 2 and 3 fell: the loop is neither 18.6 nor 24 us off.

**The sum.** The touched stages give -0.8, -1.7, +0.7, -0.4 and -0.7: -2.8 us (-3.3 in the second profile). Forgetting attention, which no edit touches, gives -3.1 and -5.4, all other stages +0.7 and +0.2. That makes the 5.2 and 8.5 us between the profiles; the rest of the 10.7 is that the kernel before was profiled 2.0 under its median, and the changed one, the first time, 3.7 over its own. So the forecast's 2107.4 is right as a number by luck, and wrong as an account: a stage that it left at nothing gave more than those that it counted. Two of its own signs of being wrong came as well, the single widening at 1.20 us and PE's clock at 0.50 where it stood at full.

Of forgetting attention's 3.1 and 5.4 us, 1.3 and 2.6 lie between its 500th and its 7300th record, where the steps stand. Another 1.6 lie ahead of the 500th record in either profile, and the rest behind the 7300th; these are not traced further. Over all profiles it took 949.7 to 953.0 us in the seven with the merge and no empty stage, and 952.6 to 957.6 in the other seven. The steps explain how an edit acts on a stage 150 us later: with the third normalization's stage gone they fall elsewhere, 3.9 us less in b, and with an empty stage in its place (k) they are back. It was said before the prediction that what a stage saves the kernel saves, and that waits don't reach into another stage; by this and by the clock at the stages' starts, that is not so. Neither do the parts add up: alone they give -0.25%, -0.23%, +0.05% and +0.29%, together -0.14% or -3 us, but the whole gives -0.55%.

## What to carry to other kernels

Work that looks redundant may be what brings PE back to its upper clock: before taking it out, look at the granted clock of what comes behind, and price that at both levels. A stage's gain is not the kernel's: the clock at which the next stage starts can change with it, worth 1.5 to 1.7 us where it did here, so four edits must be timed together. When a total agrees with a forecast, compare it stage by stage before believing the terms; and when a stage that no edit touches has changed its length, compare it record by record, since the difference may stand in a few places.

## What was not expected of the hardware

Six matmuls of 128 columns, 1.7 us of PE work with no use, went with 2.7 and 3.0 us less in the following stage (h and n; 127.3 without), whose start ran at 1.00 instead of 0.50. A 1.4 to 1.7 us longer end of a stage cost 1.7 more in the next (i). An unedited stage of 950 us differed by up to 8 us between kernels, and by 2.4 between two executions of one (952.1 and 949.8). And data that land 0.35 us later cost 1.6 us, where VectorE's instruction of 0.19 us then meets a GpSimd product of 1.27 us and takes 1.16.
